# The values of an image's seventh x tile are made one attention chunk later

## The reference, cut to what matters

```python
# layer 0, per image; x is 256 x 4096
q = Wq @ x + bq                      # 32 x 4096
k = Wk @ x + bk                      # 32 x 4096
v = Wv @ x + bv                      # 256 x 4096
attn = softmax(q.T @ k, axis=0)      # over i of scores[i, j]
x = gamma * (v @ attn) + x
# layer 1, per image
theta = theta_w @ x + theta_b        # 32 x 4096
phi = maxpool2(phi_w @ x + phi_b)    # 32 x 1024
g = maxpool2(g_w @ x + g_b)          # 128 x 1024
att = softmax(theta.T @ phi, axis=-1)
x = gamma1 * (out_w @ (g @ att.T) + out_b) + x
```

## Time and profile before

| | |
|---|---|
| median of 3 runs | 2654.15 us (2653.09 to 2655.64) |
| the profiled execution | 2652.04 us |
| its span, first to last instruction | 2650.2 us |
| TensorE busy | 2579.8 us |
| VectorE busy | 2033.6 us |
| GpSimd busy | 1942.3 us |
| ScalarE busy | 1745.2 us |

### The profile page before, as it was taken

The page is one execution under the profiler, slowest core; times in us unless marked ns, Lnnn a source line. Parts: engine busy times, 40 slices in busy tenths (PEclk is TensorE's granted clock), DMA queues, the critical chain, the costliest instruction groups (busy, mean ns, idle before and its releaser), DMA issues.

```text
span 2650.2 us, 38444 instructions
## 1 busy us (share of the span) xinstructions
PE 2579.8 (97%) x11696; PEld 2077.9 (78%) x11696; DVE 2033.6 (77%) x3384; ACT 1745.2 (66%) x3182; POOL 1942.3 (73%) x1528
## 2 busy tenths in 40 slices
PE   7999999999999999999999999999999999999978
PEld 6788888787778888877777888887777788888756
DVE  6678888777878887876887777787688778877766
ACT  6566666675776666666587666666658666666566
POOL 5677777665897777766698777776669877777667
PEclk9999999999999999999999999999999999999989
DMA  2000000110120000011022000001002100000012
GB/s 92 1 17 17 17 17 17 32 57 25 57 82 23 17 17 25 25 33 49 17 72 80 17 25 17 17 17 49 25 17 89 64 17 17 17 17 17 17 48 73
DMA packets 47658, 88.99 MB, mean 34 GB/s; under 512 B 5344, under 2 KB 5472, under 8 KB 47456
## 3 DMA queue, kind: packets, MB, share of 16 engines
q1 hardware_dynamic: 46896, 85.73, 10.0%
q10 hardware_dynamic: 560, 0.79, 0.1%
HBM read 52.70 MB, written 33.55 MB: 33 GB/s over the span
## 4 chain that ended last, share of the span: by engine, by line
PE 89%; DVE 4%; issue 2%; POOL 1%; ACT 1%; DMA 1%; SPq 1%; POOLq 0%; ACTq 0%; DVEq 0%
PE o_ps L1094 19%; PE o_ps L1091 19%; PE o_ps L1095 19%; PE aux L1128 11%; PE s_ps L1059 10%; PE aux L1105 3%; PE aux L1145 2%; PE aux L1162 2%; PE aux L1109 2%; DVE mx L908 2%; PE aux L1141 1%; PE aux L1137 1%; DVE acc L870 1%; POOL prob_l L655 1%; PE aux L1165 1%
## 5 line engine op out<-in xcount | busy, mean ns | idle before, releaser
L655 POOL TENSOR_TENSOR prob_l<-prob,prob_h 128x512 fp32r<-128x512 f32 x1280 | 1645.5, 1295 | 654.6 <-PE o_ps L1095 544.7
L714 ACT ACTIVATE prob<-s_ps 128x512 f32<-128x512 f32 x1280 | 767.2, 599 | 754.2 <-PE s_ps L1059 748.7
L908 DVE TENSOR_REDUCE mx<-aux 128x1 f32<-128x512 f32 x1257 | 859.8, 685 | 345.5 <-PE aux L1128 340.3
L1091 PE MATMUL o_ps<-prob_h,vh 128*128 128x512 f32 x2304 | 909.2, 395 | 3.7 <-ACT prob_h L717 1.3
L1094 PE MATMUL o_ps<-prob_l,vh 128*128 128x512 f32 x2304 | 903.8, 392 | 2.1 <-POOL prob_l L655 1.4
L1095 PE MATMUL o_ps<-prob_h,vl 128*128 128x512 f32 x2304 | 900.3, 391 | 0.0
L870 DVE TENSOR_TENSOR acc<-prob,acc 128x512 f32<-128x512 f32 x1187 | 814.0, 686 | 56.1 <-ACT prob L714 36.8
L717 ACT ACTIVATE prob_h<-s_ps 128x512 fp32r<-128x512 f32 x1280 | 764.9, 598 | 0.0
L1059 PE MATMUL s_ps<-queries,keys 128*128 128x512 f32 x1280 | 523.4, 410 | 25.0 <-DMA queries<-nm_turned 23.8
L1128 PE MATMUL aux<-keys,queries 128*128 128x512 f32 x1257 | 508.6, 405 | 13.0 <-DVE mx L908 8.0
L1091 PEld LDWEIGHTS o_ps<-prob_h,vh 128*128 128x128 f32 x2304 | 434.3, 188 | 104.0 <-ACT osb L728 10.6
(11 more groups left out here) (125 smaller groups left out, 1642.1 us busy)
## 6 DMA issues: line engine op xcount, KB each, us to landing
xa<-x SPq DMA_DIRECT2D x32, 512.0 KB, 3.7
xp<-x SPq DMA_DIRECT2D x32, 512.0 KB, 3.7
spill<-xa SPq DMA_DIRECT2D x32, 512.0 KB, 2.8
xa<-spill SPq DMA_DIRECT2D x32, 512.0 KB, 3.7
y<-xa SPq DMA_DIRECT2D x32, 512.0 KB, 2.8
queries<-nm_turned SPq DMA_DIRECT2D x256, 1.0 KB
xp<-spill SPq DMA_DIRECT2D x3, 512.0 KB, 4.8
prob<-w_in ACTq DMA_DIRECT2D x1, 640.0 KB, 5.6
```

Of the source, the lines that this page charges most:

```text
L655: nc.gpsimd.tensor_tensor(out=prob_l[:, i, :], in0=prob[:, i, :], in1=prob_h[:, h % RING, :].bitcast(f32), op=ALU.subtract).then_inc(pl_re ...
L714: nc.scalar.activation(prob[:, h % PRING, :], s_ps[s][:, :], ACT.Exp).then_inc(p_ready, 1)
L908: ins = nc.vector.tensor_reduce(out=dst, in_=bank[:, :], axis=AX.X, op=ALU.max)
L1091: mm(out[:, :], value(vh, l, t, ct), prob_h[:, i, :], start=t == 0, stop=False)
```

## The change

The second rounding (round 2) of x tile 6 and both of its `V0` go from the last chunk of the image before (tiles 26 to 31) to the image's own first chunk (tiles 3 to 8). Three products for maxima of the second layer make room there, from tiles 6, 8 and 10 to 9, 10 and 11. The rounded parts of the second layer's last x tile go to buffer 0, since buffer 1 holds x tile 6 then.

```diff
-           (0, 6, (18, 3), (19, 1), (20, 1)), (0, 5, (21, 3), (22, 1), (22, 3)), (0, 7, (22, 3), (23, 1), (23, 3)),
-           (2, 6, (26, 3), (27, 1), (27, 3)))
+           (0, 6, (18, 3), (19, 1), (20, 1)), (0, 5, (21, 3), (22, 1), (22, 3)), (0, 7, (22, 3), (23, 1), (23, 3)))
...
-           (4, 1, (21, 3), X2, (22, 3)), (5, 0, (24, 3), X2, (25, 3)), (5, 1, (26, 1), X2, (27, 1)),
-           (6, 0, (28, 3), X2, (29, 3)), (6, 1, (30, 1), X2, (31, 1)))
-VALUES0_NEXT = ((7, 0, (1, 1), X2, (2, 1)), (7, 1, (2, 3), X2, (3, 3)))
+           (4, 1, (21, 3), X2, (22, 3)), (5, 0, (24, 3), X2, (25, 3)), (5, 1, (26, 1), X2, (27, 1)))
+VALUES0_NEXT = ((7, 0, (1, 1), X2, (2, 1)), (7, 1, (2, 3), X2, (3, 3)),
+                (6, 0, (5, 3), X2, (6, 3)), (6, 1, (7, 1), X2, (8, 1)))
...
         if first_of_later:
+            put(g + 3, 3, Job("X", 2, b, NCH - 2, 0))
+            for k in range(CT):
+                put(g + 4, 1 + 2 * k, Job("XL", 2, b, NCH - 2, k))
             values0(g, b, VALUES0_NEXT)
...
-                         [(t, 1, X2) for t in (4, 6, 8, 10, *range(13, 25))])
+                         [(t, 1, X2) for t in (4, 9, 10, 11, *range(13, 25))])
...
     if job.l == 2:
         return 1
+    if job.l == 1 and job.c == NCH - 1 and job.b + 1 < B:
+        return 0
     return (0, 1, 1, 0, 1, 1, 0, 0)[job.c] if job.l == 0 and job.b else job.c % 2
```

## The result

The changed kernel takes **2666.3 us** (median of 7 runs, 2660.01 to 2667.47), the kernel before 2654.4 beside it; the ratio is 1.0043, with a 95% interval of 1.0034 to 1.0052. The forecast was slower, 2662.0 in a range of 2657 to 2667. So sign and range held, the range with 0.7 us to spare at its upper end, and the loss of 7.8 us came out at 11.9.

What follows compares the result with a forecast made beforehand. TensorE, busy 97% of the span, bounds the kernel, so only its waits and clock change. Cover 4.3, first-chunk wait 0.3 and clock 3.2 sum to 7.8 us on 2654.15, giving 2662.0 us, range 2657 to 2667.

Steps and rivals of the forecast that it cites:

- The wait: End of each image's last chunk: scores' wait for the maxima's DMA grows from 1.7 to 2.2 us to 3.2 to 3.6.
- the chain starts earlier: Rival: less last-chunk work on ScalarE and GpSimd starts the chain 0.71 us sooner, loss 2.2 in all, 2656.3; chance 0.06.
- The cover, 4.3 us: Last chunk: the first `V0` of x tile 6 no longer fills the scores' wait, +1.43 us per image, three times.
- The second half, ScalarE, VectorE's additions, SyncE, `x_slot`, 0: Second `V0` of x tile 6, rounding `X`, `V0L` and moved `ST`, x tile load, other x buffer: each 0.
- The load's new place: Next image's first x tile load moves from ahead of four small DMAs to the next chunk's tile 4: 0.
- The wait in the first chunk, 0.3 us: First chunk: TensorE waits 0.1 us per image for GpSimd's added `XL` pair; bounds 0 and 2.53.
- The 0.1 us for `XL`: First chunk, tile 5: GpSimd ends the pair at 1277.63, TensorE reaches the moved `V0` at 1277.56.
- The clock, 3.2 us: Clock falls to 1.2 GHz behind two of the three longer waits, 1.6 us each; bounds 0 and 4.8.
- The price of a fall: Behind a wait: 3.5 us at 1.2 GHz hold 1.6 us less work, from matmul starts 0.43 against 0.23 apart.
- nearer to 4.05: New waits of 3.2 to 3.6 us lie nearer to 4.05 (clock fell) than to 2.19 (clock held).
- the dear first chunk: Same rival as "the first chunk pays more": up to 2669 us, chance 0.12.
- the first chunk pays more: Rival: GpSimd's 2.53 us or VectorE's subtractions delay the first chunk, at most 2.53 us an image, 2669; chance 0.12.

Runs made afterwards that it cites:

- e2_behind: Kernel before, with the first `V0` of x tile 6 moved behind the new image's scores (tile 30), within the last chunk; 2663.2 us, ratio 1.0038.
- e4_cover: Kernel before, with the second `V0` of x tile 6 also ahead of the new image's waiting scores (tile 29); 2647.8 us, ratio 0.9984.
- e8_refill: Changed kernel, with the first `V0` of x tile 7 at tile 28 of the last chunk; 2656.7 us, ratio 1.0007 to the kernel before.
- e3_second: Kernel before, with only the second `V0` of x tile 6 moved to tile 5 of the next chunk; 2651.1 us, ratio 0.9993.
- e1_fill: Changed kernel, plus 12 idle products (1.43 us) in tile 29 of each image's last chunk; 2658.5 us, ratio 1.0023 to the kernel before.
- e6_fill6: e1_fill with 6 idle products instead of 12; 2661.1 us, ratio 1.0030 to the kernel before.
- e5_later: e1_fill with both `V0` of x tile 6 one tile later and three maxima products at tiles 5, 6, 11; 2658.5 us, ratio 1.0017 to kernel before.
- e9_warm: Kernel before, plus idle 128x512 products in its four longest waits, at the start and end; 2649.2 us, ratio 0.9989.
- e10_both: Kernel before with the edits of e4_cover and e9_warm together; 2644.3 us, ratio 0.9969.

## Why the prediction was right, and where it was short

- **The wait (right).** Foretold 3.6, 3.2 and 3.2 us, measured 3.22, 3.20 and 3.57; the growth in all is 4.28, foretold 4.3. TensorE's own work beside the chain shrank by 1.4 us each time, as foretold. The chain itself did not keep its length at images 1 and 3, and that its changes (-0.38, +0.05 and +0.37 us) cancel is luck. The rival "the chain starts earlier" is out: TensorE's small waits of the earlier trace rows, 0.49 and 0.22 us, are 0.48 and 0.22 in the changed kernel, so they were not for what left the chunk.
- **The cover, 4.3 us (right).** e2_behind makes the loss with the cover alone, e4_cover the gain of the same size, e8_refill takes the loss away with other work as cover.
- **The second half, ScalarE, VectorE's additions, SyncE, `x_slot`, 0 (right for what was tried).** e3_second moves the second half to tile 5 and uses the other buffer: 0. The load's new place was not tried alone, and 0 is not shown for it. At image 1 the chain from the last product for maxima to the scores takes 5.81 or 5.82 us in all five kernels with the load behind the four small DMAs, and 6.17 to 6.24 in the six others in which the scores wait for it. At image 3 it goes the other way in four of the five (5.99 to 6.20 against 5.78 or 5.79), so the sum over the images hides it; but there e2_behind, which moves no load, has 6.21 too.
- **The wait in the first chunk, 0.3 us (too small).** It is 1.6, by e1_fill (0.7 an image less the 0.2 at the first attention), and 0.5 an image again in e8_refill. The 0.1 us for `XL` was worked out from when GpSimd would be done, and measured 0.26; but the wait of the second `V0` and of the next product for maxima for the bank X2 was not in the sum at all. I counted VectorE's busy share, not how soon after a `V0` the next user of its bank comes. That TensorE has no waits between tiles 3 and 11 was wrong too: the row at 1274.03 is one.
- **The clock, 3.2 us (right in kind, too small).** It is 5.8 by e1_fill, above the upper bound of 4.8. The price of a fall was right: 1.44 and 1.65 us for the two of some 3.4 us, foretold 1.6. The clock fell behind all three waits, which was in the bounds, and at the first for 6.8 us instead of some 3.5 (2.74 us), which wasn't: one row had given one length, and I took it for the only one, though the kernel before also has low stretches of 10.2 us near its end and of 17.1 at its start. The reasoning from the length of the wait ("nearer to 4.05") led to the right side, but e6_fill6 (2.5 to 2.7, held) and e8_refill (1.79, fell) show that the length alone doesn't decide. By the price that the Trainium skill gives in "TensorE: Matmul & The Clock Gate", section "Terms", the slow time by (1 - K/N), an estimate for the 13.7 us here is 6.8 us. The 5.8 us measured between the changed kernel and e1_fill are less: 1.3 us of the slow time still lie in the waits, and the other 12.4, at the prediction's 1 - 0.23/0.43, make 5.8.
- **The sum.** 4.3 + 1.6 + 5.8 = 11.7 us in the six chunks, as measured there, where the forecast had 4.3 + 0.3 + 3.2 = 7.8. The time forecast for a clock that falls behind one to three waits, 2660.4 to 2663.6, was missed. The range held because it reached up to 2667 for another rival, the dear first chunk; that this room was enough for the longer fall and the waits for the bank is luck.
- **The rival "the first chunk pays more"** is true in its cause and false in its size: 1.6 us, not 7.2. The stated sign of it, over 4 us of growth with the clock at 1.00, did not come; in e1_fill, with the clock at 1.00, it is 1.9 to 2.1.

What stays open: why the clock falls behind one wait and not behind another, and what makes the chain at images 1 and 3 longer or shorter by 0.4 us. The differences between executions of one kernel (2 to 7.5 us here) are of the size of what the end of the kernel does: 203.0 to 207.4 us over the runs in which nothing there was changed, longer with more time at 1.2 GHz (17.7 us of it in the kernel before, 35.2 in e6_fill6). The start adds to it: its low stretch is 17.1 us in most profiles, and 10.2 in e5_later and e8_refill. So the sums of the six chunks tell the edits apart better than the medians.

## What to carry to other kernels

Where a chain through other engines and a DMA ends in TensorE's wait, an independent product that stands between its first and its last link is free, as one `V0` was here, and moving it "later, where there is room" costs its full length unless TensorE waits there too; look for such work before moving it, and stop when the wait is used up. A wait that grows by one such product can cost more by the clock behind it than by itself (5.8 against 4.3 us here), so compare with a kernel in which the gap is filled with idle products before blaming the moved work. And when jobs share a bank, look for each new place how soon the next user of the same bank comes.

## What was unexpected of the hardware

- The clock fell to 1.2 GHz at waits of 3.2 to 3.7 us each time (six of six in the changed kernel and e2_behind), at a wait of 1.79 us once (e8_refill), and at none of 2.5 to 2.7 us (three of three in e6_fill6); all of this in one profiled execution of each. The low stretch was 3.4 us in four cases and 6.8 in three, in otherwise equal places.
- Near the end of the kernel, with TensorE busy 15.05 of 23.80 us, the clock stayed low for all of it (e6_fill6). With matrix products that compute nothing it stayed up at the start in one profile (e9_warm, the stretch 58.9 to 76.0: 0.50 before, 1.00 with them) and fell for 10.2 us in another with the same products (e10_both).
- Waits of TensorE of 0.34 to 0.42 us, and one of 0.56 in e5_later, leave no idle time ahead of a matmul in the timeline, only ahead of its weight load; three of them cost 0.7 us together.
